# A gated MLP between two attentions: first product by whole sequences in three f32r products, row normalisation as one affine instruction on ScalarE

## The reference

```
h = shift_token(x)                     # half of the features from the token before
mu = h.mean(-1); var = h.var(-1)
h = (h - mu) / sqrt(var + 1e-05) * lg + lb
h = h @ w1 + b1                        # w1: 128 x 682
a, g = split(h, 2)                     # 341 columns each
h = a * gelu(g)
x = x + h @ w2 + b2                    # w2: 341 x 128
```

## Time and profile before

| | |
|---|---|
| median of 3 runs | 1178.63 us (1176.59 to 1178.84) |
| profiled execution | 1174.67 us, of it the span 1172.9 us |
| PE, DVE, ACT, POOL busy | 93%, 84%, 79%, 62% of the span |
| mean granted clock of PE | 0.98 |
| MLP 0, transposes | 426.5 to 503.7 us |
| MLP 1, transposes | 769.7 to 844.3 us |

### The profile page before, as it was taken

How to read it: one execution, slowest core, us unless ns; L and a number is a source line. 1 busy time by engine, 2 the same in 40 slices (tenths; PEclk the granted TensorE clock), 3 DMA queues, 4 the chain that set the end, 5 groups by cost and what they waited for, 6 DMA issues and landing times.

```text
span 1172.9 us, 33608 instructions
## 1 busy us (share of the span) xinstructions
PE 1088.3 (93%) x11412; PEld 922.1 (79%) x11412; DVE 989.7 (84%) x2339; ACT 924.7 (79%) x2616; POOL 730.6 (62%) x1090
## 2 busy tenths in 40 slices
PE   6899976999999989979999999989989997999996
PEld 3777754888888879967888888888867776799996
DVE  4799968999889858878899889768889997599988
ACT  4898866999999975559999999865578886876672
POOL 4799937777777744437777777634589994444431
PEclk9999989999999999999999999999999999999999
DMA  6000000111111112111112310111000000000000
GB/s 201 22 2 1 2 15 17 29 29 29 29 28 24 24 27 65 34 23 23 30 29 47 83 28 19 31 25 28 17 2 2 3 1 2 6 13 14 15 15 16
DMA packets 62408, 30.79 MB, mean 26 GB/s; under 512 B 46197, under 2 KB 56481, under 8 KB 62242
## 3 DMA queue, kind: packets, MB, share of 16 engines
q1 hardware_dynamic: 59474, 27.15, 9.7%
q10 hardware_dynamic: 2768, 1.51, 0.5%
HBM read 9.77 MB, written 2.10 MB: 10 GB/s over the span
## 4 chain that ended last, share of the span: by engine, by line
PE 63%; DVE 14%; ACT 9%; issue 8%; POOL 4%; DMA 0%; DVEq 0%; ACTq 0%; POOLq 0%
PE m_ps_y L1512 7%; PE a_ps_b L1030 5%; PE a_ps_t L1041 5%; PE a_ps_s L936 5%; PE a_ps_a L963 5%; PE a_ps_t L1005 4%; PE a_ps_qk L920 4%; DVE x_e L692 3%; PE f_ps_y L1299 3%; PE f_ps_g L1310 3%; PE a_ps_qk L921 2%; PE a_ps_qk L922 2%; PE f_ps_a L1317 2%; PE a_ps_s L977 2%; PE m_ps_h L1499 2%
## 5 line engine op out<-in xcount | busy, mean ns | idle before, releaser
L1108 ACT ACTIVATE a_e<-a_ps_s,a_stat 128x128 f32<-128x128 f32 x512 | 226.6, 477 | 3.1 <-DVE a_stat L1177 3.1
L1239 POOL TENSOR_TENSOR a_rot<-a_rot 128x512 f32<-128x512 f32 x64 | 82.7, 1293 | 136.1 <-DVE a_rot L1131 136.1
L1233 POOL TENSOR_TENSOR a_e<-a_e,a_stat 128x1024 f32<-128x1024 f32 x64 | 121.4, 1897 | 5.8 <-DVE a_stat L1156 5.8
L1108 ACT ACTIVATION_READ_ACCUMULATOR a_e<-a_ps_s,a_stat 128x1 f32 x512 | 115.7, 226 | 0.0
L1346 ACT ACTIVATE f_gl<-f_ps_g,vec 128x128 f32<-128x128 f32 (+1 forms) x192 | 55.8, 361 | 58.7 <-PE f_ps_g L1310 58.7
L1227 POOL TENSOR_TENSOR a_rot<-a_rot 128x512 f32<-128x512 f32 x64 | 81.6, 1275 | 18.2 <-DVE a_rot L1131 18.2
L1129 DVE TENSOR_TENSOR a_rot<-a_ps_qk,a_rtab 128x512 f32<-128x512 f32 x128 | 86.9, 679 | 0.0
L1131 DVE TENSOR_TENSOR a_rot<-a_ps_qk,a_rtab 128x512 f32<-128x512 f32 x128 | 86.8, 678 | 0.0
L741 DVE TENSOR_REDUCE x_stat<-x_ps_s 128x16 f32<-128x1024 f32 x64 | 77.1, 1205 | 11.4 <-PE x_ps_s L547 11.3
L1173 DVE TENSOR_REDUCE a_stat<-a_ps_s 128x8 f32<-128x1024 f32 x64 | 77.8, 1215 | 4.7 <-PE a_ps_s L936 4.5
L1166 DVE TENSOR_REDUCE a_stat<-a_sq 128x16 f32<-128x1024 f32 x64 | 78.0, 1218 | 3.5 <-ACT a_sq L1115 2.1
(11 more groups left out here) (204 smaller groups left out, 3644.1 us busy)
## 6 DMA issues: line engine op xcount, KB each, us to landing
a_vx<-a_vt SPq DMA_DIRECT2D x64, 128.0 KB, 2.3
a_h<-y SPq DMA_DIRECT2D x64, 32.0 KB
f_h<-y SPq DMA_DIRECT2D x64, 32.0 KB
out_dram<-x SPq DMA_DIRECT2D x32, 64.0 KB, 1.5
a_h<-y SPq DMA_DIRECT2D x64, 31.8 KB
f_h<-y SPq DMA_DIRECT2D x64, 31.8 KB
w<-in_L_ffn_w_dram SPq DMA_DIRECT2D x2, 768.0 KB, 5.4
x<-in_x_dram SPq DMA_DIRECT2D x1, 768.0 KB, 5.4
```

Of the source, the lines that this page charges most:

```text
L1108: act.activation(self.e[n % 2][:, P * i:P * i + P], ps_s[:, P * i:P * i + P], ACT.Exp, bias=stat[:, 24 + i:25 + i], scale=stat[:, root:roo ...
L1233: p.tensor_tensor(e3, e3, self.stat[n % UNROLL][:, 16:24].unsqueeze(2).broadcast_to([P, 8, P]), ALU.mult)\
L1239: p.tensor_tensor(r, r, self.rot2[:, INNER:], ALU.add).then_inc(self.s_n, 1)
```

## The change

- The first product works on pairs of tiles, one sequence of 256 tokens. The normalised and transposed pair is split into hTh (rounded to f32r, ACT, times lg) and hTl (the rest, DVE), w1 into w1h and w1l, and each 128 features x 256 tokens are the sum of three f32r matmuls, w1h hTh + w1l hTh + w1h hTl: 18 matmuls for each pair instead of 12 of f32 (24 passes) for two tiles.
- g is made in step n + 5 and a in step n + 6 of the odd tile n; each has now one set of two PSUM banks instead of two sets of one. Gelu and f_act have 256 columns. The second product moves from n + 7 to n + 8 and stays in f32 and by tiles.
- lb leaves the copy: w1 times lb is made once for each layer in step 3 (PE, six one-column matmuls) and added to the biases (DVE, two instructions).
- The row normalisation moves from DVE to ACT as one instruction with scale and bias from memory (`Norm.affine`); POOL makes the bias, minus mean times inverse deviation, in a third instruction (`rstd_shift`).
- w1 is split six steps ahead of the stage (PREP): two copies on ACT, two subtractions on POOL. The split weights, hTh and act lie in buffers that the first cross-attention leaves free (`kT[0]`, `vall[0]`); POOL fills their padding.
- The blocks on DVE stand in the order hTl (n + 4), f_act (n + 6), x update (n + 9), statistics (n + 2), output add (n + 8); on ACT hTh (n + 4), affine (n + 3), gelu (n + 5).

```diff
+    def rstd_shift(self, g, k, t):
+
+        g.wait_ge(self.s_st, 2 * k + 2)
+        after(g, self.s_nm, k - 1)
+        g.tensor_scalar(t[:, 8:9], t[:, 7:8], 1e-5, None, ALU.add).then_inc(self.s_rs, 1)
+        g.wait_ge(self.s_rs, 3 * k + 1)
+        g.tensor_tensor(t[:, 9:10], t[:, 8:9], self.g.neg_half, ALU.pow).then_inc(self.s_rs, 1)
+        g.wait_ge(self.s_rs, 3 * k + 2)
+        g.tensor_scalar(t[:, 10:11], t[:, 6:7], t[:, 9:10], -1.0, ALU.mult, ALU.mult).then_inc(self.s_rs, 1)
+
+    def affine(self, act, k, t, dst, src):
+        act.wait_ge(self.s_rs, 3 * k + 3)
+        act.activation(dst, src, ACT.Identity, bias=t[:, 10:11], scale=t[:, 9:10]).then_inc(self.s_nm, 1)
...
+        keys, values = g.kT[0], g.vall[0]
+        self.w1h, self.w1l = keys[:, 0:6 * P], keys[:, 6 * P:12 * P]
+        self.hTh, self.hTl = [keys[:, 12 * P + S * i:12 * P + S * i + S] for i in range(2)], self.many("hTl", 2, S, F32R)
         self.st = self.many("st", 2, 16)
-        self.gl, self.act, self.yo = self.many("gl", 2, 3 * P), self.many("act", 2, 3 * P), self.many("yo", 2, D)
+        self.gl, self.yo = self.many("gl", 2, 3 * S), self.many("yo", 2, D)
+        self.act = [values[:, 3 * S * i:3 * S * i + 3 * S] for i in range(2)]
...
+    def product(self, pe, dst, c, b, signal):
+
+        at = slice(P * c, P * c + P)
+        pe.matmul(dst, self.w1h[:, at], self.hTh[b % 2][:, :], start=True, stop=False)
+        pe.matmul(dst, self.w1l[:, at], self.hTh[b % 2][:, :], start=False, stop=False)
+        pe.matmul(dst, self.w1h[:, at], self.hTl[b % 2][:, :], start=False, stop=True).then_inc(signal, 1)
...
+        if s == 3:
             pe.wait_ge(g.s_mw, g.n_mw * (l + 1))
+            self.take(pe, l, "x")
+            for i, lo in enumerate((0, HID)):
+                for c, w in enumerate(HCH):
+                    m = pe.matmul(ps_x[1][0:w, S + 3 * i + c:S + 3 * i + c + 1], g.mw1[:, lo + P * c:lo + P * c + w], g.vec[:, 1:2],
+                                  start=True, stop=True)
+            m.then_inc(self.s_bp, 1)
         n = s - 4
+            k, u, b = T * l + n, n % 2, n // 2
             pe.wait_ge(self.ln.s_nm, k + 1)
-            after(pe, self.s_hc, k - 1)
-            if n == 0:
-                self.take(pe, l, "x")
-            pe.transpose(ps_x[u][:, 0:P], self.hn[u][:, :], g.ident).then_inc(self.s_t, 1)
-        n = s - 7
-        if 0 <= n < T:
-            k, u = T * l + n, n % 2
-            pe.wait_ge(self.s_ac, 3 * k + 3)
+            after(pe, self.s_hc, T // 2 * l + b - 1)
+            after(pe, self.s_hl, T // 2 * l + b - 1)
+            if n == 2:
+                pe.wait_ge(self.s_bf, 2 * l + 2)
+            pe.transpose(ps_x[b % 2][:, P * u:P * u + P], self.hn[u][:, :], g.ident).then_inc(self.s_t, 1)
+        n = s - 5
+        if 0 <= n < T and n % 2:
+            b, q = n // 2, T // 2 * l + n // 2
+            pe.wait_ge(self.s_hc, q + 1)
+            pe.wait_ge(self.s_hl, q + 1)
+            after(pe, self.s_gl, 3 * q)
+            if b == 0:
+                pe.wait_ge(self.s_wh, 2 * l + 2)
+                pe.wait_ge(self.s_wl, 2 * l + 2)
+                pe.wait_ge(self.s_z, 8)
+                self.take(pe, l, "g")
+            for c in range(3):
+                self.product(pe, ps_g[:, S * c:S * c + S], c, b, self.s_g)
+        n = s - 6
+        if 0 <= n < T and n % 2:
+            b, q = n // 2, T // 2 * l + n // 2
+            after(pe, self.s_ac, 3 * q)
+            if b == 0:
+                self.take(pe, l, "a")
+            for c in range(3):
+                self.product(pe, ps_a[:, S * c:S * c + S], 3 + c, b, self.s_a)
+        n = s - 8
+        if 0 <= n < T:
+            k, u, b = T * l + n, n % 2, n // 2
+            pe.wait_ge(self.s_ac, 3 * (T // 2 * l + b) + 3)
             after(pe, self.s_yc, k - 1)
...
+        if s == PREP:
             act.wait_ge(g.s_mw, g.n_mw * (l + 1))
+            act.wait_ge(self.cross.s_up, T)
+            after(act, self.s_a, 3 * T // 2 * l)
+            act.activation(self.w1h[:, 0:HID], g.mw1[:, HID:2 * HID], ACT.Copy).then_inc(self.s_wh, 1)
+            act.activation(self.w1h[:, 3 * P:3 * P + HID], g.mw1[:, 0:HID], ACT.Copy).then_inc(self.s_wh, 1)
...
+        if 0 <= n < T and n % 2:
+            k, b, q = T * l + n, n // 2, T // 2 * l + n // 2
             act.wait_ge(self.s_t, k + 1)
-            after(act, self.s_g, k - 1)
-            after(act, self.s_a, k - 1)
-            act.activation(self.hT[u][:, :], ps_x[u][:, 0:P], ACT.Identity, bias=g.vec[:, 1:2], scale=g.vec[:, 0:1])\
-                .then_inc(self.s_hc, 1)
+            after(act, self.s_a, 3 * (q - 1))
+            act.activation(self.hTh[b % 2][:, :], ps_x[b % 2][:, 0:S], ACT.Copy, scale=g.vec[:, 0:1]).then_inc(self.s_hc, 1)
+        n = s - 3
+        if 0 <= n < T:
+            after(act, self.s_t, T * l + n - 1)
+            self.ln.affine(act, T * l + n, self.st[n % 2], self.hn[n % 2][:, :], self.h[n % UNROLL][:, :])
         n = s - 5
-        if 0 <= n < T:
-            k, u = T * l + n, n % 2
-            act.wait_ge(self.s_g, k + 1)
-            after(act, self.s_ac, 3 * (k - 1))
+        if 0 <= n < T and n % 2:
+            b, q = n // 2, T // 2 * l + n // 2
+            after(act, self.s_ac, 3 * (q - 1))
+            if b == 0:
+                act.wait_ge(self.s_bf, 2 * l + 2)
             for c, w in enumerate(HCH):
-                act.activation(self.gl[u][0:w, P * c:P * c + P], ps_g[u][0:w, P * c:P * c + P], ACT.Gelu,
+                act.wait_ge(self.s_g, 3 * q + max(c, 1) + 1)
+                act.activation(self.gl[b % 2][0:w, S * c:S * c + S], ps_g[0:w, S * c:S * c + S], ACT.Gelu,
                                bias=g.vec[0:w, 5 + c:6 + c]).then_inc(self.s_gl, 1)
...
+        if s == 3:
             v.wait_ge(g.s_mw, g.n_mw * (l + 1))
-            v.wait_ge(self.s_z, 4)
+            v.wait_ge(self.s_z, 8)
+            v.wait_ge(self.s_bp, l + 1)
+            bias = g.vec[:, 2:8].rearrange("p (i c) -> p i c", c=3)
+            more = ps_x[1][:, S:S + 6].rearrange("p (i c) -> p i c", c=3)
+            for rows, c in ((slice(0, P), slice(0, 2)), (slice(0, HCH[2]), slice(2, 3))):
+                v.tensor_tensor(bias[rows, :, c], more[rows, :, c], bias[rows, :, c], ALU.add).then_inc(self.s_bf, 1)
+            v.wait_ge(self.s_bf, 2 * l + 2)
+        n = s - 4
+        if 0 <= n < T and n % 2:
+            b, q = n // 2, T // 2 * l + n // 2
+            v.wait_ge(self.s_hc, q + 1)
+            after(v, self.s_a, 3 * (q - 1))
+            v.scalar_tensor_tensor(out=self.hTl[b % 2][:, :], in0=ps_x[b % 2][:, 0:S], scalar=g.vec[:, 0:1], in1=self.hTh[b % 2][:, :],
+                                   op0=ALU.mult, op1=ALU.subtract).then_inc(self.s_hl, 1)
         n = s - 6
-        if 0 <= n < T:
-            k, u = T * l + n, n % 2
-            v.wait_ge(self.s_gl, 3 * k + 3)
-            v.wait_ge(self.s_a, k + 1)
-            after(v, self.s_y, k - 1)
+        if 0 <= n < T and n % 2:
+            b, q = n // 2, T // 2 * l + n // 2
+            after(v, self.s_y, 2 * (q - 1))
             for c, w in enumerate(HCH):
-                at = slice(P * c, P * c + P)
-                v.scalar_tensor_tensor(out=self.act[u][0:w, at], in0=ps_a[u][0:w, at], scalar=g.vec[0:w, 2 + c:3 + c],
-                                       in1=self.gl[u][0:w, at], op0=ALU.add, op1=ALU.mult).then_inc(self.s_ac, 1)
-        n = s - 3
-        if 0 <= n < T:
-            after(v, self.s_t, T * l + n - 1)
-            self.ln.norm(v, T * l + n, self.st[n % 2], self.hn[n % 2][:, :], self.h[n % UNROLL][:, :])
+                at = slice(S * c, S * c + S)
+                v.wait_ge(self.s_gl, 3 * q + c + 1)
+                v.wait_ge(self.s_a, 3 * q + max(c, 1) + 1)
+                v.scalar_tensor_tensor(out=self.act[b % 2][0:w, at], in0=ps_a[0:w, at], scalar=g.vec[0:w, 2 + c:3 + c],
+                                       in1=self.gl[b % 2][0:w, at], op0=ALU.add, op1=ALU.mult).then_inc(self.s_ac, 1)
         n = s - 9
         if l and 0 <= n < T:
             v.wait_ge(self.s_yc, T + n + 1)
             v.scalar_tensor_tensor(out=tok(g.x, n), in0=self.yo[n % 2][:, :], scalar=g.tg[:, 2:3], in1=tok(g.x, n),
                                    op0=ALU.mult, op1=ALU.add).then_inc(self.s_up, 1)
+        n = s - 2
+        if 0 <= n < T:
+            k = T * l + n
+            v.wait_ge(self.s_d[n % UNROLL], landed(k))
+            self.ln.stats(v, k, self.st[n % 2], self.h[n % UNROLL][:, :])
...
+            for i, (at, lo) in enumerate(((0, HID), (3 * P, 0))):
+                p.wait_ge(self.s_wh, 2 * l + i + 1)
+                p.tensor_tensor(self.w1l[:, at:at + HID], self.g.mw1[:, lo:lo + HID], self.w1h[:, at:at + HID], ALU.subtract)\
+                    .then_inc(self.s_wl, 1)
         n = s - 2
         if 0 <= n < T:
-            self.ln.rstd(p, T * l + n, self.st[n % 2])
+            self.ln.rstd_shift(p, T * l + n, self.st[n % 2])
```

More of the change, by code:

```diff
@@ L36 @@
 UNROLL = 4
+PREP = -6
 AWAY = -2.0e38
```

(39 more changed lines are left out.)

21 lines of the change are left out of this document (8 added, 13 removed).

## The result

The changed kernel takes 1221.80 us (median of 4 runs, 1220.14 to 1223.34), the kernel before 1178.74 beside it (4 runs). The ratio is 1.0366, 95% interval 1.0342 to 1.0389: 43.1 us slower. 1207 was forecast, with 1187 to 1224. In the profiled executions the span went from 1172.9 to 1220.4 us (+47.5), at a mean granted clock of 0.982 and 0.969.

The account below looks back on a forecast made before the run. PE and, in layer 1, a normalisation loop bound the MLP before; a longer ScalarE-VectorE-POOL loop would after. Layer 0 14.1, layer 1 12.8, ends 3, preparation 1: +30.9 us, forecast 1207, range 1187 to 1224.

Parts of the forecast that it names:

- forecast case: Both MLP stretches slowed by the new closed loop; 1207 us, own range 1197 to 1217, chance 0.68.
- the ends: Ends of the MLP stages: +1.5 us a layer, bounds -1 and +4.
- the preparation: Rounding w1 six steps ahead, in attention, hidden by ScalarE's free 0.3 us; +1 us both layers, bounds 0 and 5.
- The deciding step: MLP: norm on ScalarE closes a loop through ScalarE, VectorE and POOL; 5.44 us a pair, layer 1 5.71.
- The end of layer 0's stretch: Next layer's weight rounding on ScalarE, on the loop, about 1.37 us; layer 0 in all +14.1 us.
- Layer 1's experts: Two of four expert weight roundings on ScalarE stand on the loop, +0.9 us; layer 1 in all +12.8.
- Rival 1: MLP: hTh and hTl stay off the loop; faster, 1164 to 1168 us, or 1159 to 1163 PE-paced; chance 0.13.
- second half: Rival 1's PE-paced case: PE's 3.85 us a pair sets the pace of both layers, 1159 to 1163 us.
- Rival 2: PE loses its clock in the MLP's new gaps; a quarter of pairs cold about +9, 1216 us; chance 0.12.
- Rival 3: 256-column matmuls in the MLP get no cheaper, 0.23 us each; PE 5.7 us a pair, 1211; chance 0.04.
- the 0.216: Skill-based estimate for each new 256-column matmul with its weight load: 0.216 us, 5.4 us a pair on PE.
- Rival 4: No change: smaller sums and the norm's vanished POOL-VectorE stalls give back what the loop costs; chance 0.03.

Follow-up runs that it names:

- e1: Changed kernel with VectorE's statistics block moved ahead of hTl instead of behind f_act and the x update; 1177.2 us, ratio 0.9984.
- e5: Changed kernel with POOL's last instruction of rstd_shift issued twice, the second waiting for the first; 1231.8 us, ratio 1.0453.
- e2: Changed kernel with normalisation back on VectorE and two POOL instructions, so the pair product alone; 1202.6 us, ratio 1.0223.
- e6: Kernel before with only the normalisation moved to ScalarE as an affine and three POOL instructions, products by single tiles; 1177.4 us, ratio 0.9990.
- e10: Changed kernel with eight buffers for the shifted tiles instead of four; 1221.8 us, ratio 1.0385.
- e3: Changed kernel with POOL's two w1l subtractions moved from step -6 to steps -5 and -4; 1216.1 us, ratio 1.0327.
- e7: e4 with fillings and subtractions moved into POOL's idle gap in attention steps, and ScalarE's two roundings in two steps; 1169.4 us, ratio 0.9932.
- e8: e7 with eight buffers for the shifted tiles instead of four; 1163.2 us, ratio 0.9873.
- e4: Changed kernel with the moves of e1 and e3 together; 1171.9 us, ratio 0.9952.

## Why the prediction was right, and where it was short

The direction and the mechanism were right, and the stretches came within 3.1 and 2.1 us. The total is less well hit than the wide range suggests: 1221.8 lies 4.8 us above the forecast case's own range of 1197 to 1217. The range up to 1224 was drawn for a slower clock and for the ends, and it is luck that it also took in the preparation, which passed its own bounds.

- **The deciding step held.** 5.44 and 5.71 us a pair were added up from the trace of before; 5.46 and 5.76 came. Term by term, start to start, in layer 0: affine 0.40 (0.38 forecast), gelus 1.07 (1.11), hTh to hTl 0.49 (0.54), hTl to f_act 0.41 (0.39), f_act 1.17 (1.17), stats to aggregate 0.31 (0.32), to POOL 0.28 (0.27), POOL 0.31 and 0.67 (0.30 and 0.67), to the affine 0.35 (0.29). e1 shows that the loop is the cause, e5 that GpSimd is on it once a pair, e2 and e6 that this loop needs both parts.
- **The end of layer 0's stretch was short by 1.6 us.** Its last pair takes 8.49. Of the excess, 1.37 is the next layer's a_wqh on ScalarE ahead of hTh, as forecast. The rest is GpSimd, in the timeline of the changed kernel (VectorE's line first, from the same window of time):

```profile
520.98 1.75 DVE L1166 TENSOR_TENSOR a_wqr<-wqkv,a_wqh 128x1536 fp32r<-128x1536 f32 x1
```

```profile
520.97 1.83 POOL L277 TENSOR_SCALAR f_st<-f_st 128x1 f32<-128x1 f32 x1 [4.34 <-DVE f_st L264]
```

  An instruction on one column takes 1.83 us instead of 0.23 and ends 0.07 us after a_wqr, whose two inputs lie in SBUF. The Trainium skill ("SBUF — State Buffer", section "SBUF: two separate sides") calls the port pair that VectorE and GpSimd share an exclusive lock: between a VectorE instruction with two SBUF inputs and a GpSimd instruction that reads SBUF, the one that starts first holds it for its whole length. The trace agrees in the blocking; which of the two started first, 0.01 us apart in the records, it cannot say. The prediction let a_wqr "fall into the step in which it has two microseconds to spare". VectorE had them; GpSimd, on the loop, had not. The timelines of the kernel before already show it, 1.64 us long and ending 0.08 us after VectorE's:

```profile
500.71 1.73 DVE L1151 TENSOR_TENSOR a_wqr<-wqkv,a_wqh 128x1536 fp32r<-128x1536 f32 x1
```

```profile
500.88 1.64 POOL L268 TENSOR_SCALAR f_st<-f_st 128x1 f32<-128x1 f32 x1 [1.44 <-DVE f_st L263]
```

  The other 1.5 us between 14.1 and 17.2: the loop 0.3, pairs of 5.53 and 5.69 0.3, and the single step left beside 13 pairs, which takes 3.62 and not half a pair, 0.9.
- **Layer 1's experts cost more.** 12.8 forecast, 14.9 measured. 0.7 is the loop (13.5 x 0.05). The pairs with expert roundings or next-stage work, 6.17, 6.18, 5.88 and 6.42, are together 1.6 us above 5.76, where 0.9 was allowed; the single step gives another 0.7.
- **The preparation was the mis-sized term:** +1 us for both layers, bounds 0 and 5; it cost 8.0 in the profiled execution, and 6.4 in those of e1 and e10, where layer 0 kept its clock. The prediction also named added time in the attention as a sign of being wrong, and a sixth of it lies there. Two things were missed. ScalarE's free 0.3 us of an attention step is no place where two copies can hide when GpSimd waits for them; and GpSimd's subtractions were taken as work beside the others, though they stand ahead of the a_rot and a_e that PE waits for. The prediction named GpSimd's list but did not ask who waits behind it. e3 takes away the wait for ScalarE, e7 also the place ahead of a_e.
- **The ends** were put at 3 us, bounds -2 and 8; 3.9 is what the profiled executions show, and their scatter is as large.
- **The rivals.** Rival 1 (faster) did not come, since hTh and hTl do join the loop. e1 and e8 open the loop in another place, and there its second half holds: PE's 3.7 us a pair sets the pace, and e8 took 1163.2 us where 1159 to 1163 was its forecast. Its 3.85 was a little high, since a matmul of 256 columns follows at 0.12 and not at 0.127. Rival 2 came in part and cost nothing where it was looked for: in layer 1 the granted clock was 0.91 in the stretch, and undisturbed pairs stayed within 5.75 to 5.77, since PE is not on the loop. It cost 1.6 us in layer 0's preparation step, of which the rival did not speak. Rival 3 is excluded by the 0.12, and so is the 0.216 that the prediction set beside its own 0.127. Rival 4 (no change) is excluded by the 43.1.

In sum 30.9 was forecast for the profiled execution and 47.5 measured: +3.1 and +2.1 in the stretches, +7.0 in the preparation, +0.9 at the ends, 3.5 not explained. The median came 14.8 us over the forecast; the preparation is the largest part of that.

## What to carry to other kernels

Before moving work between engines, write down every closed chain from a tile to the tile one period later, through the order of each engine's list; the sums of work fell on PE, VectorE and ScalarE here and the time rose 3.7%, and moving one block to the head of its list took it all back. For work that is added "in idle time", look at the instruction that stands behind it and at who waits for that one, not at the engine's free share. And after a loop is opened, look again: here the weights' subtractions and then the depth of the loads came up as the next bounds: the time went to 0.998 of that before, then to 0.993, then to 0.987 (the last step helps the kernel before as well, by 0.2%).

## What the runs showed of the hardware

- f32r matmuls of 128 x 256, each with a fresh load of 128 x 128 weights, follow each other at 0.12 us at full clock (0.11 for an f32 pass of 128 columns).
- A GpSimd instruction of one column lasts 1.83 us beside a VectorE instruction of 1536 columns with two SBUF inputs (1.64 in the kernel before), 0.23 without.
- After 2.40 us of idle PE, f32r matmuls of 512 columns took 0.43 us, in a stretch with a granted clock of 0.85; in e10, with the same code in that step, after 2.41 us, they took 0.23 at 1.00.
- A loop that idles PE for about a quarter of the time kept 1.00 in layer 0 (PE 55.57 of 77.93 us) and had 0.91 in layer 1 (61.01 of 80.10).
- A load of one shifted tile took 6.37 us to land during the MLP of layer 0 (e4), longer than the three steps that four buffers give it at 4 us a pair.
